# Where the first batch's output-weight remainders and conditioning tables are made

## What is computed

```python
def ada_rmsnorm(x, t, gamma_w, beta_w):
    return (t @ gamma_w.T)[:, None, :] * rmsnorm(x) + (t @ beta_w.T)[:, None, :]

# layer 0: attention with 16 heads of 16, then a gated feed-forward, 1024 wide
x = x + (t @ attn_alpha_w.T)[:, None, :] * attention(ada_rmsnorm(x, t, ...), W_q, W_k, W_v, W_o)
h = ada_rmsnorm(x, t, ...)
x = x + (t @ ffn_alpha_w.T)[:, None, :] * (silu(h @ gate_w.T) * (h @ hidden_w.T) @ out_w.T + out_b)
# layer 1: rmsnorm scaled by cond @ norm_w.T + 1, up projection, gelu gate,
# 8-bit rounding of the activations, ternary down weights, residual
```

## Time and profile before

| | us |
|---|---|
| median of 3 runs | 1073.39 |
| lowest and highest | 1072.73, 1075.54 |
| the profiled execution, its own time | 1073.16 |
| its span | 1071.4 |
| TensorE busy | 1025.2 |
| VectorE busy | 751.5 |
| ScalarE busy | 577.0 |
| GpSimd busy | 367.2 |
| granted clock of TensorE, mean of the span | 0.988 of full |

### The profile page before, as it was taken

The page is one execution under the profiler, slowest core; times in us unless marked ns, Lnnn a source line. Parts: engine busy times, 40 slices in busy tenths (PEclk is TensorE's granted clock), DMA queues, the critical chain, the costliest instruction groups (busy, mean ns, idle before and its releaser), DMA issues.

```text
span 1071.4 us, 19375 instructions
## 1 busy us (share of the span) xinstructions
PE 1025.2 (96%) x6775; PEld 717.6 (67%) x6775; DVE 751.5 (70%) x1527; ACT 577.0 (54%) x1282; POOL 367.2 (34%) x431
## 2 busy tenths in 40 slices
PE   7689999999999999999999999989989999999997
PEld 6334367756765775677577667745868788888775
DVE  5776876677668567766866776676647786756775
ACT  5276785576567556755766685565652333332221
POOL 2511143433343343324333343222333443534331
PEclk9799999999999999999999999999999999999999
DMA  8224232024113212411231222030311111011111
GB/s 270 83 84 129 64 105 80 22 72 138 32 37 110 81 32 66 140 51 31 90 106 32 66 85 84 23 106 2 100 54 32 59 50 41 30 45 55 59 50 40
DMA packets 81312, 75.96 MB, mean 71 GB/s; under 512 B 13008, under 2 KB 79576, under 8 KB 81216
## 3 DMA queue, kind: packets, MB, share of 16 engines
q1 hardware_dynamic: 79184, 72.82, 21.9%
q10 hardware_dynamic: 2032, 1.90, 0.6%
HBM read 53.29 MB, written 21.39 MB: 70 GB/s over the span
## 4 chain that ended last, share of the span: by engine, by line
PE 81%; DVE 8%; issue 5%; DMA 3%; POOL 2%; ACT 1%; SPq 0%; POOLq 0%; ACTq 0%; DVEq 0%
PE gen L1212 32%; PE core L1212 12%; PE pvb L1342 11%; PE core L1301 9%; PE core L1330 8%; DVE negmax L967 4%; PE gen L1559 2%; PE gen L1286 1%; PE pvb L1551 1%; PE pvb L1350 1%; DMA shift_d<-shift 1%; DMA parts_d<-qk 1%; DMA xa<-x_d 1%; POOL v L676 1%; PE gen L1382 1%
## 5 line engine op out<-in xcount | busy, mean ns | idle before, releaser
L967 DVE TENSOR_REDUCE negmax<-core 128x1 f32<-128x512 f32 x512 | 340.0, 685 | 159.0 <-PE core L1301 158.2
L742 ACT ACTIVATE p<-core 128x512 f32<-128x512 f32 x512 | 279.0, 599 | 127.0 <-PE core L1330 125.5
L1212 PE MATMUL gen<-hs,wgh 128*128 128x256 f32 x1536 | 218.7, 292 | 0.5 <-POOL hs L569 0.5
L1212 PEld LDWEIGHTS gen<-hs,wgh 128*128 128x128 f32 x1536 | 193.8, 189 | 35.9 <-DVE shift L980 10.9
L1301 PE MATMUL core<-kst,qst 96*128 96x512 bf16 x512 | 199.2, 392 | 17.3 <-DVE negmax L967 14.7
L1212 PE MATMUL core<-wup,hp 128*128 128x512 f32 x768 | 190.1, 396 | 2.0 <-POOL hp L668 2.0
L612 POOL TENSOR_TENSOR a<-a 128x256 fp32r<-128x256 f32 x128 | 95.2, 744 | 271.8 <-ACT a L760 269.1
L1212 PEld LDWEIGHTS core<-wup,hp 128*128 128x128 f32 x768 | 139.7, 188 | 30.2 <-issue 2.0
L1330 PE MATMUL core<-qst,kst 99*128 99x512 bf16 x512 | 157.1, 385 | 2.9 <-DMA qst<-shift_d 1.5
L1342 PE MATMUL pvb<-p,v 128*32 128x512 f32 x1024 | 123.9, 602 | 0.0
L1212 PE MATMUL gen<-wout,a 128*128 128x256 f32 x768 | 113.8, 284 | 1.4 <-DVE h L961 0.7
(11 more groups left out here) (163 smaller groups left out, 1207.2 us busy)
## 6 DMA issues: line engine op xcount, KB each, us to landing
qst<-parts_d SPq DMA_DIRECT2D x192, 64.0 KB, 2.3
kst<-parts_d SPq DMA_DIRECT2D x187, 64.0 KB, 2.3
parts_d<-qk SPq DMA_DIRECT2D x30, 384.0 KB, 2.7
xr<-in_x_dram SPq DMA_DIRECT2D x8, 512.0 KB, 4.0
x_d<-x SPq DMA_DIRECT2D x8, 512.0 KB, 3.2
xa<-x_d SPq DMA_DIRECT2D x32, 128.0 KB, 2.3
v<-x_d SPq DMA_DIRECT2D x32, 128.0 KB, 2.2
out_dram<-v SPq DMA_DIRECT2D x32, 128.0 KB, 1.7
```

Source lines behind the costliest of these rows:

```text
L742: act.activation(p32[:, ring(b, m), k * S:(k + 1) * S], stb[k], ACT.Exp, scale=SCALE).then_inc(s["exp_"], 1)
L967: dve.tensor_reduce(negmax[:, n // TT, n % TT:n % TT + 1], smb[n % 2], AX_X, ALU.max, negate=True).then_inc(s["smax"], 1)
L1212: last = pe.matmul(out_, l, r, start=start and i == 0, stop=stop and i == len(passes) - 1, **kw)
```

## The change

It touches the first batch alone.

- **Low parts of `wout`.** In steps 18 to 21, VectorE's four `split_lo` are gone. ScalarE copies each turned bank twice: to `hi`, and whole as float32 (`whole_weights`) into `h32` and `o`, which are not in use then. GpSimd subtracts (`wout_low`), one step later in its stream.
- **Tables on TensorE.** `Z_REST` goes from 22 to 25, so that the ten transposes stand behind all of the first 16 score matmuls and ahead of the turn of the maxima, and the products, two steps on, behind the 20th score matmul.
- **Tables off VectorE.** ScalarE copies the products out (`copy_tables`); GpSimd adds 1 to the norm table and multiplies the row (`finish_tables`). VectorE keeps the column copy of batch 1, now `next_table(1)` in step 30.
- **Waits.** TensorE's wait for all low parts becomes one for the nine of VectorE and, for the banks, one for ScalarE's copies (`wout_f`). The wait for GpSimd's parts stands at the start of iteration 0.
- GpSimd's `memset` of `v1` moves behind batch 1's normalising, as it hangs on `Z_REST`.

```diff
-    Z_REST = 22
+    Z_REST = 25
+    N_LATE = 9
     for n in range(4):
-        W_TURN[T_MAX + n] = W_HI[T_MAX + n] = W_LO[T_MAX + n] = (9 + n, 10 + n)
+        W_TURN[T_MAX + n] = W_HI[T_MAX + n] = (9 + n, 10 + n)
...
+            def wout_low(g):
+                pool.wait_ge(s["wt_hi"], g + 1)
+                pool.wait_ge(s["wout_f"], g - N_LATE + 1)
+                hi, lo = WG[g][1]
+                pool.tensor_tensor(lo, wout_f32[g - N_LATE], hi.bitcast(F32), ALU.subtract).then_inc(s["wout_lo"], 1)
+
+            def finish_tables():
+                nt = NSC * KD
+                pool.wait_ge(s["tab2_copy"], 1)
+                norm = table[:, nt - KD:nt, :].rearrange("p n b -> p (n b)")
+                pool.tensor_scalar(norm, norm, 1.0, None, ALU.add).then_inc(s["tab2_copy"], 1)
+                pool.wait_ge(s["row_copy"], 1)
+                pool.wait_ge(s["ob_load"], 16)
+                pool.tensor_tensor(arow[:, 2 * D:3 * D], arow[:, D:2 * D], obrow[:, :], ALU.mult).then_inc(s["row_ob"], 1)
...
+                    if i == -1 and z - 1 in W_HI and W_HI[z - 1][0] >= N_LATE:
+                        wout_low(W_HI[z - 1][0])
+                    if i == -1 and z == Z_REST + 4:
+                        finish_tables()
...
+            def whole_weights(g):
+                act.copy(wout_f32[g - N_LATE], first_bank[g][:, :]).then_inc(s["wout_f"], 1)
+            def copy_tables():
+                nt, nf = NSC * KD, NFIRST * KD
+                act.wait_ge(s["tab2_mm"], 1)
+                act.copy(table[:, nf:nt, :].rearrange("p n b -> p (n b)"), gen[1][:, 0:(nt - nf) * B]).then_inc(s["tab2_copy"], 1)
+                act.wait_ge(s["row_mm"], 1)
+                act.copy(arow[:, 0:2 * D], gen[0][0:B, :]).then_inc(s["row_copy"], 1)
...
+                    if i == -1 and z == Z_REST + 3:
+                        copy_tables()
...
-            def other_tables():
-
-                dve.wait_ge(s["tab2_mm"], 1)
-                dve.tensor_copy(table[:, nf:nt - KD, :].rearrange("p n b -> p (n b)"), gen[1][:, 0:(nt - KD - nf) * B]).then_inc(s["tab2_copy"], 1)
-
-                dve.tensor_scalar(table[:, nt - KD:nt, :].rearrange("p n b -> p (n b)"), gen[1][:, (nt - KD - nf) * B:(nt - nf) * B], 1.0, None, ALU.add).then_inc(s["tab2_copy"], 1)
-                dve.wait_ge(s["row_mm"], 1)
-                dve.tensor_copy(arow[:, 0:2 * D], gen[0][0:B, :]).then_inc(s["row_copy"], 1)
...
-                    if i == -1 and z == Z_REST + 4:
-                        other_tables()
+                    if i == -1 and z == Z_REST + 5:
+                        dve.wait_ge(s["tab2_copy"], 2)
+                        next_table(1)
...
                 if step == 0:
-                    pe.wait_ge(s["wt_lo"], len(WG))
+                    pe.wait_ge(s["wt_lo"], N_LATE)
+                    pe.wait_ge(s["wout_f"], len(WG) - N_LATE)
...
                     if i == 0 and z == 0:
-                        pe.wait_ge(s["wt_lo"], len(WG))
+                        pe.wait_ge(s["wout_lo"], len(WG) - N_LATE)
+                        pe.wait_ge(s["tab2_copy"], 1)
+                        pe.wait_ge(s["row_copy"], 1)
```

More of the change, by code:

```diff
@@ L200, in build @@
         qs = sb("qs", [P, TT, 4])
+        o_flat = o[:, :, :].rearrange("p t d -> p (t d)")
+        wout_f32 = [h32[:, n, :] for n in range(KD)] + [o_flat[:, n * S:(n + 1) * S] for n in range(2)]
         stage_q = qst[:, :, :].rearrange("p h t -> p (h t)").bitcast(F32)
@@ L241, in build @@
         tab_mm tab_copy tab2_mm tab2_copy stack_first first_qh first_qm first_kh first_km first_kl qkv_t qkv_hi qkv_lo row_mm row_copy row_ob alpha_stored kones
-        wt_t wt_hi wt_lo cur_set cur2_set
+        wt_t wt_hi wt_lo wout_f wout_lo cur_set cur2_set
         xa_load xr_load al_load sq1 ms1 rs1 xn1 xt1 h32_1 hh1 hl1
@@ L834, in iteration @@
                         split_hi(WG, "wt_t", "wt_hi", first_bank, *W_HI[z])
+                        if W_HI[z][0] >= N_LATE:
+                            whole_weights(W_HI[z][0])
                     if i == -1 and z == T_QK[1] + 2:
@@ L912, in _ @@
             dve.tensor_copy(a32_flat[0:C, 0:NFIRST * D], core_flat[0:C, 0:NFIRST * D]).then_inc(s["cw_tc"], 1)
-            nt, nf = NSC * KD, NFIRST * KD
+            nf = NFIRST * KD
             def first_tables():
@@ L920, in first_tables, with next_table @@
                 dve.tensor_copy(cur[:, 0, 0:nf].unsqueeze(2), table[:, 0:nf, bass.ds(0, 1)]).then_inc(s["cur_set"], 1)
-            def other_tables():
-                dve.wait_ge(s["tab2_mm"], 1)
-                dve.tensor_copy(table[:, nf:nt - KD, :].rearrange("p n b -> p (n b)"), gen[1][:, 0:(nt - KD - nf) * B]).then_inc(s["tab2_copy"], 1)
-                dve.tensor_scalar(table[:, nt - KD:nt, :].rearrange("p n b -> p (n b)"), gen[1][:, (nt - KD - nf) * B:(nt - nf) * B], 1.0, None, ALU.add).then_inc(s["tab2_copy"], 1)
-                dve.wait_ge(s["row_mm"], 1)
-                dve.tensor_copy(arow[:, 0:2 * D], gen[0][0:B, :]).then_inc(s["row_copy"], 1)
-                dve.wait_ge(s["row_copy"], 1)
-                dve.wait_ge(s["ob_load"], 16)
-                dve.tensor_tensor(arow[:, 2 * D:3 * D], arow[:, D:2 * D], obrow[:, :], ALU.mult).then_inc(s["row_ob"], 1)
+            def next_table(b):
+                dve.tensor_copy(cur[:, 0, :].unsqueeze(2), table[:, :, bass.ds(b, 1)]).then_inc(s["cur_set"], 1)
             def split_lo(gs, hi_sem, lo_sem, banks, g0=0, g1=None):
@@ L1094, in iteration @@
                             first_tables()
-                        else:
-                            if b == 1:
-                                dve.wait_ge(s["tab2_copy"], 2)
-                            dve.tensor_copy(cur[:, 0, :].unsqueeze(2), table[:, :, bass.ds(b, 1)]).then_inc(s["cur_set"], 1)
+                        elif b > 1:
+                            next_table(b)
                     for b in at(z, T_H1):
```

## The result

| | median of runs, us | runs | ratio to the kernel before, in the same session |
|---|---|---|---|
| before | 1073.87 | 22 | |
| changed | 1071.05 (lowest 1068.44, highest 1075.97) | 22 | 0.9972 [0.9959, 0.9985] |
| changed, a second session | 1071.32 | 12 | 0.9970 [0.9954, 0.9985] |

The change makes the kernel faster by about 0.3%: a small gain, but its interval leaves out 1 in both sessions. Forecast were 1072.2 and a gain of 1.0 to 1.2 us; measured were 1071.05 and 2.8 (the difference of the medians). The profiled execution of the changed kernel took 1072.51 us, its span is

The account below looks back on a forecast made before the run. TensorE, busy nearly throughout, bounds the kernel. Early fall: 40.4 + 3.57 + 0.6 + 4.66 + 2.00 = 51.2, late 50.1, against 51.37; middle 0.7, plus 0.3 for the clock: 1073.16 becomes 1072.2, range 1068.5 to 1075.1.

Parts of the forecast that it names:

- The path: First batch, first maxima to first score matmul of the second kind: maxima without holes, then products, not the DMA, last.
- the turn: Turn of the first 16 maxima: at 39.3, or 40.4 if the clock falls early, where it was at 44.39.
- the last stretch: Behind the products, score matmuls 21 to 23 and a maximum, up to the first second-kind score matmul: 2.00 us.
- The chance of 0.77: Chance given for the measured time to lie within the stated bounds; faster than 1070.2 got 0.20, slower than 1076.6 got 0.03.
- left one path and stand on the next: Products, formerly ahead of the turn, now stand behind it ahead of the first second-kind score matmul: 7.95 at the lower price.
- The stall of VectorE: Cut of the shift behind the turn: VectorE's cast held by GpSimd's subtraction, 0.6 us added to 3.57.
- the 1.85: Time from the turn to the start of SyncE's store of the shift, read before; included a cast stall of 0.26.
- rival (2): Cut of the shift: GpSimd stalls cast and L980, 1.9 in all, clock falls early; 1074.7 to 1075.1, chance 0.14.
- The clock at the products: Behind the turn, narrow products and row run at 1.2 GHz whether the clock falls early or late: 4.66, not 2.38.
- The base: Starting time for the gain: profiled execution of before at 1073.16, median of its runs 1073.39.
- (1): Clock stays at 2.4 GHz through transposes and products; 4.1 to 4.7 gained, 1068.5 to 1069.1, chance 0.16.
- (3): The 5 us are given back later at a sparse place against the clock's fall, about 1.5 each; 1073 to 1074, chance 0.08.

Follow-up runs that it names:

- e1_noprod: Changed kernel with its products cut to one narrow one and one of 8 columns, so later numbers are not the reference's; 1068.26 us, ratio 0.9936.
- e1_fill: Changed kernel plus 20 transposes nobody reads, four in each of steps 22 to 24 and eight in step 26; 1073.06 us, ratio 0.9983.
- e2_split: Changed kernel with the row product one step later, behind score matmuls 21 and 22; 1071.93 us, ratio 0.9970.
- e1_lowparts: Kernel before with only the low parts of wout moved off VectorE, tables left as before; 1072.08 us, ratio 0.9985.
- e2_fill2: Changed kernel plus 28 transposes nobody reads, four in each of steps 22 to 24 and sixteen in step 26; 1071.23 us, ratio 0.9968.
- e2_after: Changed kernel again without any edit, in a second session, with a second profile; 1071.32 us, ratio 0.9970.
- e3_early_lo: Changed kernel with transposes in step 14, narrow products in 22 and 23, row in 25, and low parts back on VectorE; 1070.53 us, ratio 0.9980.
- e3_early: Changed kernel with condition transposes in step 14, narrow products in 22 and 23, row product in 25, measured again; 1070.45 us, ratio 0.9964.
- e3_row24: Changed kernel with condition transposes in step 14, narrow products in 22 and 23, row product in 24; 1070.12 us, ratio 0.9953.

## Why the prediction was right, and where it was not

**The path (right).** The maxima ran without a hole (16 in 9.79 and 10.13), the turn came at 40.41 and 40.44 where 40.4 stood for a clock that falls early (and at 39.6 with the clock held, where 39.3 stood), the last stretch took 1.93 where 2.00 stood, and no DMA came last. The chance of 0.77 at the end of the prediction goes with 1070.2 to 1076.6, which is 0.3% to either side of before, and not with the range of 1068.5 to 1075.1 that stands beside it. That the products "left one path and stand on the next" is what e1_noprod shows.

**The stall of VectorE (over-sized).** The stretch from the turn to the products was put at 3.57 + 0.6; it took 3.04 and 3.26. In both profiles of the changed kernel the cast L1007 began 0.5 behind the end of GpSimd's last subtraction, and the power and the normalisations behind it held nothing. The other 0.3 to 0.5 were in the 1.85 taken over from before, which already held the stall of 0.26 and a slower turn. The mechanism exists: 0.70 in e1_fill. It needed a turn some 0.8 earlier, at 39.6, which came with the clock up and not with the early fall that rival (2) joined it to. The prediction's own numbers say as much: with the turn at 40.4 and 1.04 from the turn to the cast, as in the earlier trace rows, the cast begins at 41.4, behind the 41.0 at which it had the subtractions end, so the 0.6 had no ground in that case. In e1_noprod, with a turn at 10.1 as in e1_fill, the cast began 0.06 behind the last subtraction and took 0.22.

**The clock at the products (mis-sized by half the cases).** "In both cases the products run at 1.2 GHz" was the step that failed. Of the two profiles of the changed kernel, one has them at 2.66 + 1.80 = 4.46 (forecast 4.66), the other at 1.43 + 1.80 = 3.23, since the clock had come back at 41.4. I had reckoned with one fall and one return; there were two of each. In e2_split, with the same instructions up to there, the narrow ones took 2.35. The same holds for the transposes: of the four executions with this order (two of the changed kernel, e2_split, e1_noprod) two had them at 1.2 GHz and two at 2.4. The sum against the first profile: 51.2 forecast, less 1.1 for the cut and the stall, less 1.4 for the narrow products, less 0.1 for the last stretch, is 48.6, as measured. Against the second it is 51.2 less 0.9, 0.2 and 0.1: 50.1, as measured (50.09).

**The base (most of the rest of the difference).** I set the sum against one profiled execution of 1073.16 and three runs, and took them as typical. 108 runs of before have a mean of 1075.0, 1.8 above the first and 1.6 above the median of the three. The profile of before was a favourable one: both products at 2.4 GHz, the clock's fall just behind them. In e1_lowparts, where the tables stand at the same place, it fell elsewhere, and the row took 1.80. So the absolute forecast, 1072.2, missed the mean of the changed kernel (34 runs, 1071.7) by only 0.5, while the gain, 1.2 forecast against the median of three, is 3.3 by the means of all runs [2.5, 4.1] (2.7 and 3.7 in the two sessions that had both kernels): 1.6 of the missing 2.1 is the base. That 1072.2 came so near is luck in part: a base that was too low and a gain that was too small cancelled. This is a comparison of means; which falls of the clock make up the 1.8 in the kernel before was not profiled.

**The rivals.** (1), the clock stays up throughout: in neither profile of the changed kernel. Nearest to it came e2_fill2, with the products at 2.38, and it gained nothing by it. (2), slower by GpSimd: no. (3), given back later: in part, 1.6 of 3.1 us in the first profile, in the stretch at 65 us, in line with the 1.5 that was allowed for each such place; the second profile had none.

## What to carry to other kernels

Work that is taken from ahead of a wait lands ahead of the next one: a move pays in full only if it ends where its engine would wait anyway, and the place can be found in the profile of before (here the wait for the first load of `kst`, 1.16 us on TensorE). Where two pieces of work feed the same wait, try each alone and both together, since the one that stays can hold what the other frees; here the runs show this for the tables alone (0.6 gained of 3.0) and leave it open for the low parts. And where the clock's falls differ from run to run, one profile is one draw: look at a second, and at the mean of many runs of the kernel before, ahead of forecasting a few tenths of a per cent.

## What the hardware showed that I had not expected

- **The scatter of the runs goes with the clock.** Over the 22 runs of the changed kernel, time and mean granted clock are tied with a correlation of 0.91: about 1061.7 + 817 x (1 - clock) us; for the kernel before (59 runs) about 1063.7 + 778 x (1 - clock), 0.88. A hundredth of the clock goes with 8 us, more than the change is worth, and most of the scatter from 1068.4 to 1076.0 follows it. The mean is not all: the two profiles of the changed kernel both have 0.988 and are 2.8 us apart, and one run of e1_fill took 1082.56 at 0.94, where the line would have 1110.7.
- **The fall comes at another place in each execution, and the return too.** For the same program the clock fell at 38.0 and 44.8 in one profile and at 35.9 in the other; in e1_lowparts it fell at 31.0, 1.4 behind the end of TensorE's wait of 1.89 for the first load, and was back at 34.5. The Trainium skill ("TensorE: Matmul & The Clock Gate", "Part 1: The HAM clock gate") has a throttled default state that activity releases. By that rule the transposes should bring it back, and in the first profile they did, at 41.4. In e2_after the same dense stretch, 38.3 to 41.7, was followed by 14 us more at 1.2 GHz. The same instructions in the same order gave both, so the order of the work alone doesn't forecast it.
- **VectorE's small operations beside GpSimd.** The cast took 0.91 beside GpSimd's subtraction in e1_fill and 0.51 in e3_early_lo beside its small multiplication of the row; and L1009, the operation that had 0.28 in all 32 cases of before, took 0.53 in e3_early and 0.36 in e3_row24 beside GpSimd's normalising. The 32 undisturbed cases were no proof that it cannot be held: by the timelines, only 7 of them had an instruction of GpSimd beside them. Nor is the stall regular. In e1_lowparts the cast and the subtraction behind it took 0.21 and 0.28 in the midst of the same normalising, beside which the cast of before took 0.47.
